# Two waits on GpSimd, and another order for the last batch, in a kernel of attention and gated graph convolution

## What is computed

```python
h = jnp.maximum(_layernorm(x), 0.0)
Wh = h @ W
e = (Wh @ a1)[:, :, None] + (Wh @ a2)[:, None, :]
e = jnp.where(e > 0, e, 0.2 * e)
e = jnp.where(adj > 0, e, -9e15)
x = x + elu(softmax(e, axis=2) @ Wh)
h = jnp.maximum(_layernorm(x), 0.0); h0 = h
A = (adj != 0)
for i in range(3):
    g = A @ (h @ weight[i])
    i_r, i_z, i_n = split(g @ w_ih.T + b_ih); h_r, h_z, h_n = split(h @ w_hh.T + b_hh)
    r = sigmoid(i_r + h_r); z = sigmoid(i_z + h_z)
    n = tanh(i_n + r * h_n)
    h = (1 - z) * n + z * h
return x + h
```

## Time and profile before

| | us |
|---|---|
| median of 3 runs | 665.85 (665.58 to 666.39) |
| profiled execution | 666.63 |
| its span | 664.8 |
| mean granted clock of TensorE, as a share of 2.4 GHz | 0.995 |

### The profile page before, as it was taken

The page is one execution under the profiler, slowest core; times in us unless marked ns, Lnnn a source line. Parts: engine busy times, 40 slices in busy tenths (PEclk is TensorE's granted clock), DMA queues, the critical chain, the costliest instruction groups (busy, mean ns, idle before and its releaser), DMA issues.

```text
span 664.8 us, 9041 instructions
## 1 busy us (share of the span) xinstructions
PE 623.5 (94%) x2969; PEld 465.4 (70%) x2969; DVE 532.1 (80%) x1238; ACT 450.2 (68%) x776; POOL 252.1 (38%) x267
## 2 busy tenths in 40 slices
PE   4988899998999989998999989999899999999895
PEld 3986667676667767676686766777666776867674
DVE  5999886899679997799958987789977998558455
ACT  4976778586776776587685867768766777644343
POOL 2214534244452435245341453523453442414440
PEclk9999999999999999999999999999999999999998
DMA  7304240214201241113402142021501032001001
GB/s 229 127 33 128 84 138 0 97 33 151 71 32 65 64 158 33 43 54 96 130 29 91 37 127 96 15 82 39 185 32 33 32 96 65 0 1 32 1 1 32
DMA packets 28366, 46.35 MB, mean 70 GB/s; under 512 B 1640, under 2 KB 19360, under 8 KB 28320
## 3 DMA queue, kind: packets, MB, share of 16 engines
q1 hardware_dynamic: 26960, 45.12, 21.2%
q10 hardware_dynamic: 1360, 0.66, 0.4%
HBM read 41.55 MB, written 4.22 MB: 69 GB/s over the span
## 4 chain that ended last, share of the span: by engine, by line
PE 61%; DVE 23%; ACT 9%; issue 4%; POOL 1%; DMA 1%; DVEq 0%; ACTq 0%; POOLq 0%
PE ps_x L1099 15%; PE ps_g L1135 14%; PE ps_x L1077 6%; DVE score L740 3%; DVE zh L840 3%; PE ps_r L1144 3%; DVE zh L847 2%; PE ps_r L1146 2%; PE ps_r L1145 2%; DVE hkT L834 2%; PE ps_z L1144 2%; PE ps_z L1145 2%; PE ps_z L1146 2%; ACT nn L472 2%; PE ps_x L1118 2%
## 5 line engine op out<-in xcount | busy, mean ns | idle before, releaser
L1135 PE MATMUL ps_g<-edges,h_hi 128*128 128x512 f32 x384 | 157.0, 409 | 9.1 <-DVE h_lo L856 7.1
L1135 PE MATMUL ps_g<-edges,h_lo 128*128 128x512 f32 x384 | 151.0, 393 | 0.0
L425 ACT ACTIVATE score<-score,nmax 128x1024 f32<-128x1024 f32 x64 | 73.9, 1154 | 44.3 <-DVE nmax L740 43.8
L1099 PE MATMUL ps_x<-probT,h_nat 128*128 128x512 f32 x224 | 98.9, 595 | 0.0
L314 POOL TENSOR_SCALAR tz<-tz 128x512 f32<-128x512 f32 x32 | 22.4, 699 | 190.4 <-ACT tz L466 190.4
L1135 PEld LDWEIGHTS ps_g<-edges,h_hi 128*128 128x128 f32 x384 | 72.2, 188 | 29.1 <-DVE h_lo L856 13.1
L740 DVE CUSTOM_DVE_ANT_0 score<-score,away 128x1024 f32<-128x1024 f32 x64 | 81.2, 1269 | 2.6 <-ACT score L419 1.8
L1135 PEld LDWEIGHTS ps_g<-edges,h_lo 128*128 128x128 f32 x384 | 72.3, 188 | 13.8
L1099 PEld LDWEIGHTS ps_x<-probT,h_nat 128*128 128x128 f32 x224 | 41.9, 190 | 50.3 <-issue 46.9
L432 ACT ACTIVATE probT<-ps_x 128x512 f32<-128x512 f32 x122 | 66.9, 597 | 12.8 <-PE ps_x L1077 12.8
L285 POOL TENSOR_SCALAR rstd<-mv 128x4 f32<-128x4 f32 (+1 forms) x25 | 11.8, 472 | 164.4 <-DVE mv L782 134.6
(11 more groups left out here) (153 smaller groups left out, 1356.4 us busy)
## 6 DMA issues: line engine op xcount, KB each, us to landing
adj_in<-in_adj SPq DMA_DIRECT2D x64, 512.0 KB, 3.4
out<-nn SPq DMA_DIRECT2D x16, 256.0 KB, 2.3
x_nat<-in_x SPq DMA_DIRECT2D x7, 512.0 KB, 4.5
ej<-ej_kept_at SPq DMA_DIRECT2D x6, 512.0 KB, 3.4
x_nat<-in_x SPq DMA_DIRECT2D x2, 256.0 KB, 3.8
probT<-in_L_gnn_weight ACTq DMA_DIRECT2D x1, 192.0 KB, 6.8
probT<-in_L_gnn_w_ih ACTq DMA_DIRECT2D x1, 192.0 KB, 7.0
probT<-in_L_gnn_w_hh ACTq DMA_DIRECT2D x1, 192.0 KB, 9.0
```

Source lines behind the costliest of these rows:

```text
L425: act.activation(score[t % U][:], score[t % U][:], ACT.Exp, bias=nmax[:, t:t + 1], scale=-1.0, accum_out=rowsum[:, t:t + 1]).then_inc(exp_ ...
L1099: last = pe.matmul(bank_of("agg", c, par)[:], h_nat[par][:, j, :], probT[:, j, :], start=(j == 0), stop=(j == T - 1))
L1135: last = pe.matmul(ps_g[c][:], part[:, s, :], edges[par][:, s, cols(c)], start=(s == 0 and part is h_hi), stop=(s == T - 1 and part is h_lo))
```

## The change

GpSimd gets two more waits. In layer 0 of every batch, the split of the first half of layer 1's input waits for `lo_done`, which VectorE raises when the second h_lo of that layer is made. At a body's end the split of the next batch's second half waits for `hk_done` of layer 2's second half. In `first`, the split of the first half moves ahead of the second rstd.

In the last batch the order of the queues changes. TensorE transposes layer 1's first state ahead of the last product of that layer (`h_back` inside `gates_g`), and its second state in the middle of the next neighbour sum. The last half of layer 2 has a function of its own, `last_gates`: r first, then hn, in, and z last. ScalarE follows that order and does the last tanh of n in two pieces of 256 nodes. VectorE takes r times hnb and the sum with ps_in (`last_in`, two pieces) ahead of the first half's state, makes the last state in two pieces (`last_state`), and adds x1 to it in two pieces (`last_out`). SyncE stores the last half in two pieces.

```diff
@@ -262,13 +264,16 @@
                     load_x(b + 3)
-                for c in range(2):
+                for c in range(2 if attend else 1):
                     sp.wait_ge(out_done, b * 2 + c + 2)
                     sp.dma_start(out_v[b, c], out_sb[c]).then_inc(stored[c], 16)
+                for q in range(0 if attend else 2):
+                    sp.wait_ge(out_done, b * 2 + q + 3)
+                    sp.dma_start(out_v[b, 1][:, 2 * q:2 * q + 2, :], out_sb[1][:, 2 * q:2 * q + 2, :]).then_inc(stored[1], 16)

...
             for c in range(2):
-                sp.wait_ge(stored[c], 16 * B + 1)
+                sp.wait_ge(stored[c], 16 * (B + c) + 1)

@@ -334,8 +339,8 @@
                 rstd2_half(0, 0)
+                split_h(0, 0, 0)
                 rstd2_half(0, 1)
-                split_h(0, 0, 0)
                 split_h(0, 0, 1)
@@ -344,6 +349,8 @@
                     z_times_h(b, l, 1)
+                    if l == 0:
+                        pool.wait_ge(lo_done, b * QH + 2)
                     split_h(b, l + 1, 0)
@@ -352,6 +359,7 @@
                     split_h(b + 1, 0, 0)
+                    pool.wait_ge(hk_done, b * QS + QS)
                     split_h(b + 1, 0, 1)
@@ -603,16 +611,22 @@
                 z_gate(b, 2, 0)
-                hnb_half(b, 2, 1)
-                if not attend:
+                if attend:
+                    hnb_half(b, 2, 1)
+                    r_gate(b, 2, 1)
                     n_gate(b, 2, 0)
-                r_gate(b, 2, 1)
-                if attend:
+                    z_gate(b, 2, 1)
+                    h0_half(a, a_par, 1)
+                    n_gate(b, 2, 1)
+                else:
+                    r_gate(b, 2, 1)
                     n_gate(b, 2, 0)
-                z_gate(b, 2, 1)
-                if attend:
-                    h0_half(a, a_par, 1)
-                n_gate(b, 2, 1)
+                    hnb_half(b, 2, 1)
+                    z_gate(b, 2, 1)
+                    for q in range(2):
+                        act.wait_ge(last_pre, q + 1)
+                        act.activation(nn[1][:, q * 2 * P:(q + 1) * 2 * P], pre[1][:, q * 2 * P:(q + 1) * 2 * P], ACT.Tanh,
+                                       bias=bih_in[:, 2:3]).then_inc(last_n, 1)
                 if prepare:
@@ -848,6 +862,36 @@
                                          ).then_inc(hk_done, 1)
+
+            def quarter(q):
+                return slice(q * 2 * P, (q + 1) * 2 * P)
+
+            def last_in(b):
+                dve.wait_ge(rh_done, b * QS + QS)
+                dve.wait_ge(in_ps, b * QS + QS)
+                for q in range(2):
+                    dve.tensor_tensor(pre[1][:, quarter(q)], pre[1][:, quarter(q)], ps_in[:, quarter(q)], ALU.add
+                                      ).then_inc(last_pre, 1)
+
+            def last_state(b):
+                for q in range(2):
+                    dve.wait_ge(last_n, q + 1)
+                    dve.tensor_tensor(zh[1][:, quarter(q)], hkT[:, HALF + q * 2 * P:HALF + (q + 1) * 2 * P], nn[1][:, quarter(q)],
+                                      ALU.subtract).then_inc(last_z, 1)
+                    if q == 0:
+                        dve.wait_ge(tz_done, b * QS + QS)
+                    dve.wait_ge(last_z, 2 * q + 1)
+                    dve.scalar_tensor_tensor(zh[1][:, quarter(q)], tz[1][:, quarter(q)], 1.0, zh[1][:, quarter(q)], ALU.add,
+                                             ALU.mult).then_inc(last_z, 1)
+                    dve.wait_ge(last_z, 2 * q + 2)
+                    dve.scalar_tensor_tensor(hkT[:, HALF + q * 2 * P:HALF + (q + 1) * 2 * P], zh[1][:, quarter(q)], 0.5,
+                                             nn[1][:, quarter(q)], ALU.mult, ALU.add).then_inc(last_done, 1)
+
+            def last_out(b, par):
+                for q, bk in enumerate((ps_r, ps_g[0])):
+                    dve.wait_ge(last_ps, q + 1)
+                    dve.tensor_tensor(out_sb[1][:, 2 * q:2 * q + 2, :], bk[:, 0:2 * P].rearrange("p (t f) -> p t f", t=2),
+                                      x1[par][:, TH + 2 * q:TH + 2 * q + 2, :], ALU.add).then_inc(out_done, 1)

@@ -994,15 +1038,19 @@
                     last_diff(b, 0)
+                    dve.wait_ge(hnb_done, b * QS + QS)
+                    r_times_hn(b, 2, 1)
+                    last_in(b)
                     last_h(b, 0)
-                    n_input(b, 2, 1)
                 if prepare:
                     scores(b + 2, 0)
-                last_diff(b, 1)
-                last_h(b, 1)
-                if not attend:
+                if attend:
+                    last_diff(b, 1)
+                    last_h(b, 1)
+                else:
+                    last_state(b)
                     out_half(b, par, 0)
-                    out_half(b, par, 1)
+                    last_out(b, par)

@@ -1201,11 +1249,33 @@
                 product(ps_z[:], of_g(1), g, False, True).then_inc(z_ps, 1)
-                if l == 0 and c == 1:
-                    h_back(b, 0, 0)
+                if c == 1 and (l == 0 or l == 1 and b + 1 == B):
+                    h_back(b, l, 0)
                 if c == 1:
...
                 product(ps_in[:], of_g(2), g, True, True).then_inc(in_ps, 1)
+
+            def last_gates(b):
+
+                n = b * QS + 2 * L
+                c, l = 1, L - 1
+                g = (g_hi[c][:], g_lo[c][:])
+
+                def of_g(k):
+                    return cT_hi[:, l, tile_cols(k)], cT_lo[:, l, tile_cols(k)]
+
+                h = part_of_h(b, l, c)
+                pe.wait_ge(tr_done, n - 1)
+                product(ps_r[:], whh(0), h, True, False)
+                pe.wait_ge(g_lo_done, n)
+                product(ps_r[:], of_g(0), g, False, True).then_inc(r_ps, 1)
+                pe.wait_ge(hnb_done, n - 1)
+                product(ps_hn[:], whh(2), h, True, True).then_inc(hn_ps, 1)
+                pe.wait_ge(pre_done, n - 1)
+                product(ps_in[:], of_g(2), g, True, True).then_inc(in_ps, 1)
+                pe.wait_ge(tz_done, n - 1)
+                product(ps_z[:], whh(1), h, True, False)
+                product(ps_z[:], of_g(1), g, False, True).then_inc(z_ps, 1)

@@ -1285,13 +1355,14 @@
                 gates_g(b, 1, 1)
-                if not attend:
-                    h_back(b, 1, 0)

...
                 if not attend:
+                    neighbours(b, par, 2, 0, 1, range(0, TH // 2))
                     h_back(b, 1, 1)
-                neighbours(b, par, 2, 0, 1)
+                    neighbours(b, par, 2, 0, 1, range(TH // 2, TH))
+                else:
+                    neighbours(b, par, 2, 0, 1)
                 if attend:
@@ -1315,15 +1386,21 @@
                 gates_g(b, 2, 0)
-                gates_h(b, 2, 1)
-                gates_g(b, 2, 1)
+                if attend:
+                    gates_h(b, 2, 1)
+                    gates_g(b, 2, 1)
+                else:
+                    last_gates(b)
                 if attend:
...
                     h_back(b, 2, 0)
-                    h_back(b, 2, 1)
+                    pe.wait_ge(last_done, 1)
+                    transposes(ps_r, [hkT[:, tile_cols(TH + t)] for t in range(TH // 2)], last_ps)
+                    pe.wait_ge(last_done, 2)
+                    transposes(ps_g[0], [hkT[:, tile_cols(TH + t)] for t in range(TH // 2, TH)], last_ps)

```

2 lines of the change are left out of this document (added).

## The result

| | before | changed |
|---|---|---|
| median, 22 runs each | 666.25 us | 667.25 us (666.64 to 669.2) |
| ratio | | 1.0018, 95% interval 1.0012 to 1.0024 |
| profiled execution, its span | 666.63, 664.8 us | 667.23, 665.2 us |

The change costs 1.0 us. I had forecast 665.6, a gain of 0.3 that nobody could tell from nothing, so the sign is wrong. The profile shows the mechanism as forecast nearly everywhere. What went wrong is a small difference of two large terms that is paid five times over, and the issue of the last store.

What follows compares the result with a forecast made beforehand. TensorE, busy 94%, was taken to bound the kernel, with waits for second states and VectorE's score 4 chain. Terms +0.6, +1.15, -0.65, -0.45, -0.97, +0.3, -0.3 gave -0.3 off 665.85: 665.6 us, range 660.0 to 669.5.

Steps and rivals of the forecast that it cites:

- gate wait, batch 0: Layer 0 to 1: state 1.35 earlier, but VectorE's run to score 4 is 2.50 longer; net 1.15 us later.
- boundary wait, batches 0 to 5, each: Between batches: layer 2's second state comes 1.39 earlier, of which TensorE takes 0.9 (0.92 in the sum).
- both, batches 1 to 5, sum: Steady batches: 1.15 lost after layer 0 less 0.92 gained between batches, +0.23 us each, +1.15 together.
- batch 6: No norm in its chain; the probT copies hold TensorE next: 1.05 less 0.23 and 0.15, taken as -0.65 us.
- boundary to batch 7: TensorE's weight loads stand idle 0.46 us before the last batch; removing that was taken as -0.45.
- last batch, layer 0: No scores stand behind the split, so the state comes in 0.69 instead of 1.66: -0.97 us.
- layer 1 and the end: Last batch: layer 1's new order +0.3 us, the last half with its stores -0.3.
- The end: Last half: last sum at 661.7 instead of 662.06, half-sized stores landing faster but close together: -0.3 us, bounds -0.9 and +0.4.
- The start: GpSimd splits the first half before the second rstd, freeing h_hi: gain 0 to 0.85 us, taken 0.55.
- VectorE pays less: GpSimd's turns fall partly beside PSUM reads, two splits cost 1.82 instead of 2.98: 658.4 us, chance 0.24.
- whole-instruction blocking: Each GpSimd instruction keeps VectorE out for its full length, both splits cost 3.86: 671.6 us, chance 0.17.
- The steady batches' cancelling: Score 4's lateness only equals the gain between batches, batches 0 to 6 give about zero: 664.4 us, chance 0.14.

Runs made afterwards that it cites:

- the better kernel: The changed kernel with edge tiles 3 to 6 moved behind the score of tile 6: 649.46 us, ratio 0.9756 to the kernel before.

## Why the prediction was wrong

Step by step, from one place of the trace to the next:

| step | forecast | changed kernel | alone |
|---|---|---|---|
| gate wait, batch 0 | +1.15 | +1.19 | +1.20 |
| boundary wait, batches 0 to 5, each | -0.92 | | -0.87 to -0.91 |
| both, batches 1 to 5, sum | +1.15 | +1.95 | |
| batch 6 | -0.65 | -0.49 | |
| boundary to batch 7 | -0.45 | -0.45 | -0.45 |
| last batch, layer 0 | -0.97 | -0.97 | -0.97 |
| layer 1 and the end | 0.0 | +0.26 | +0.3 (median +0.6) |

- **The step that failed** is "batches 1 to 5: 1.15 - 0.92 = +0.23 each". Each term was off by 0.05 only (1.20 and 0.87; the prediction has 0.9 for the boundary in one place and 0.92 in the sum), but the difference then is 0.33, and the trace has 0.34 or 0.35 in four of the five. With the gate wait alone, counted from layer 0's first transposes, the h_lo of batch 5 ends 1.34 earlier (taken 1.35), but score 4 ends 7.12 after it, not 7.07. The boundary's term is smaller by the 0.05 to 0.08 that is lost at the second transposes. Batch 4 pays 0.56, and the gate wait alone shows the same 0.2 more there. The kernel before has the reason, VectorE in batch 4:

```profile
389.32 0.69 DVE L827 SCALAR_TENSOR_TENSOR nn<-tz,nn 128x512 f32<-128x512 f32 x1 [0.38 <-ACT nn L472]
390.05 1.66 DVE L834 TENSOR_TENSOR hkT<-zh,nn 128x512 f32<-128x512 f32 x1
```
The first of the two instructions waits there for ScalarE's tanh and lasts 0.69, not the 0.92 of the other steady batches, so the gate wait has 0.97 to take off in place of 1.20. Why the tanh is late in that batch, in both kernels, is not settled. Together this step is 0.8 of the 1.3 us between the forecast of -0.3 and the measured +1.0.
- **The end** was mis-sized by 0.2: the last sum ends as early as forecast (-0.36), but I took half-sized stores to land faster, and three close together to cost only a little more than that. The half-sized stores land no sooner, and the last one is issued 0.34 after its sum, behind SyncE's issue of the one before. Layer 1 came out at +0.36, taken +0.3.
- **Batch 6** gave 0.16 less than forecast; the cause stays open.
- **The start** can't be read from these profiles. At the first transposes the kernels whose start is that of before stand -1.24, -1.22, -0.92, -0.38, +1.12 and +1.34 us from it. The changed kernel's -1.08 is inside that spread. h_hi takes 0.43 there in place of 1.26, which is the mechanism (-0.55 was taken); its worth in time is not shown.
- **The sum's base** added to it: three runs had put the median of before at 665.85, and 22 put it at 666.25, which is 0.4 of the 1.65 us between 665.6 and 667.25. The profiled execution of before is 0.4 above that median, so the traces show less of the loss than the medians.
- **The rivals.** That VectorE pays less is wrong for this run of instructions (7.11 against 7.07 says that all of it is paid), and whole-instruction blocking is wrong in its size (a turn of hT_hi takes 0.47 or 0.48 of VectorE's time and one of hT_lo 1.14, where they last 0.62 and 1.29 undisturbed; with full lengths the run would be 7.95). The rule quoted from the Trainium skill (SBUF — State Buffer, "SBUF: two separate sides") is borne out on who waits for whom in the stretches shown here: each waits for the other's instruction to end. Only the price is lower, by some 0.15 per turn. The steady batches' cancelling was nearest in kind.
- **What I did not use** is that the chain does not end at score 4. The prediction itself follows it on to the score of tile 6, but it did not ask which of VectorE's work on the way nobody waits for yet: the edge tiles. The forecast did not hang on this, the better kernel did.

## What to carry to other kernels

Where a net effect is the difference of two terms that are nearly equal and paid many times, its sign is not forecast: try each edit alone, which here showed -5.6 and +6.7 us behind +1.1 in the traces (medians -5.3, +8.0 and +0.7). A wait that keeps two engines apart in one place moves their meeting to another. Behind the boundary it fell beside reads of PSUM and cost nothing, behind the gate into a run that a chain hangs on. Look at what stands in the new place, and clear that of work which nobody waits for. Here moving four edge tiles, which by itself is worth nothing that can be told, turned the same change from a loss of 1.0 us into a gain of 16.6.

## What the runs showed of the hardware that I had not expected

- Shortening the run of VectorE that meets GpSimd saved more than the instructions taken out: 2.72 us for two edge tiles of 0.60 each, because two of GpSimd's instructions then fell behind the run, one of them beside VectorE's reads of PSUM (1.30 in place of 1.61).
- Executions of kernels with the same start stand up to 2.6 us apart at the first transposes (-1.24 to +1.34 against before), while they nearly keep their distance after that (the kernel with the last batch's edits alone stays between -1.22 and -1.06 up to the last batch, the one with the last half's edits alone goes from +1.12 to +1.51).
- Two stores of 128 KB, issued close behind one of 256 KB, take 2.2 and 2.4 us to land, as long as 256 KB alone (2.3). SyncE is busy 0.50 us with the issue of each, against 0.37 for the last store of 256 KB, and issues the next only behind it.
